# Two-layer cross-attention kernel: seven tiles of 512 rows and one of 256 instead of eight of 512, another order of the first loads and of the slot arithmetic, and two transposes placed ahead of the last gate product

## The reference, cut to what matters

```python
# layer 0, for each of 32 batches
proj = memory @ W_mem.T                                  # 375 x 512
p = softmax(x @ proj.T / sqrt(512)); mc = p @ proj
x = rmsnorm(x + sigmoid(concat(x, mc) @ W_gate.T + b) * mc)
# layer 1: a token is of expert v if it and the next one have mask 1, else of expert l
n = rms_norm(x)
qkv = where(is_v, n @ v_qkv, n @ l_qkv)                  # 512 -> 1536
q, k = apply_rotary(q, k)                                # 16 heads of 32, causal
h = x + where(is_v, ctx @ v_dense, ctx @ l_dense)
c = cross_attention(rms_norm(h) @ cq_w, encoder @ ckv_w) # 16 heads of 16
h = h + c @ cdense_w
out = h + where(is_v, mlp_v(rms_norm(h)), mlp_l(rms_norm(h)))  # 512 -> 1376 -> 512, silu(gate)*up
```

## Time and profile before

| | |
|---|---|
| median of three runs | 2606.43 us |
| profiled execution | 2607.21 us, span 2605.4 us |
| PE busy | 2340.3 us, 90% of the span |
| DVE, ACT, POOL busy | 48%, 41%, 33% |
| mean granted TensorE clock | 0.948 |
| bytes moved | 301.01 MB, 116 GB/s |

### The profile page before, as it was taken

The page is one execution under the profiler, slowest core; times in us unless marked ns, Lnnn a source line. Parts: engine busy times, 40 slices in busy tenths (PEclk is TensorE's granted clock), DMA queues, the critical chain, the costliest instruction groups (busy, mean ns, idle before and its releaser), DMA issues.

```text
span 2605.4 us, 46600 instructions
## 1 busy us (share of the span) xinstructions
PE 2340.3 (90%) x19458; PEld 1993.2 (77%) x19458; DVE 1251.0 (48%) x1871; ACT 1070.4 (41%) x1825; POOL 859.5 (33%) x720
## 2 busy tenths in 40 slices
PE   3798996999969997997999999998599999999998
PEld 2688885888858887886777777776488888888887
DVE  3455543877536663443565555565133433343332
ACT  2343424434235653442454544444334343343432
POOL 2110104666412211432121111110255646555553
PEclk7899997999979997998899999999799999999999
DMA  5343333456353333553111111110433434333341
GB/s 169 111 129 104 130 98 129 179 208 227 135 188 115 115 115 134 225 197 130 32 43 40 39 44 37 45 37 16 147 113 124 152 109 150 126 133 128 106 117 46
DMA packets 105681, 301.01 MB, mean 116 GB/s; under 512 B 14136, under 2 KB 18072, under 8 KB 98072
## 3 DMA queue, kind: packets, MB, share of 16 engines
q1 hardware_dynamic: 88128, 233.73, 27.5%
q0 software_dynamic: 17344, 64.30, 6.7%
HBM read 224.19 MB, written 73.79 MB: 114 GB/s over the span
## 4 chain that ended last, share of the span: by engine, by line
PE 80%; DVE 7%; ACT 5%; DMA 4%; issue 3%; POOL 1%; SPq 1%; POOLq 0%; DVEq 0%; ACTq 0%
PE ps L97 18%; PE ps L99 18%; PE ps L98 18%; PE ps L1048 4%; PE ps L1485 3%; PE ps L1469 3%; PE ps L1450 3%; PE ps L546 2%; ACT f_arena L1374 2%; DVE r_arena L162 2%; PE ps L1037 2%; DMA f_arena<-weights 2%; PE ps L1026 1%; PE ps L1021 1%; PE ps L1010 1%
## 5 line engine op out<-in xcount | busy, mean ns | idle before, releaser
L97 PE MATMUL ps<-r_arena 128*128 128x512 f32 (+5 forms) x2472 | 931.1, 377 | 49.9 <-DVE r_arena L604 23.3
L99 PE MATMUL ps<-r_arena 128*128 128x512 f32 (+5 forms) x2472 | 916.0, 371 | 0.0
L98 PE MATMUL ps<-r_arena 128*128 128x512 f32 (+5 forms) x2472 | 916.0, 371 | 0.0
L162 POOL TENSOR_TENSOR r_arena<-f_arena,r_arena 128x512 fp32r<-128x512 f32 (+1 forms) x438 | 581.7, 1349 | 929.1 <-ACT r_arena L184 482.5
L97 PEld LDWEIGHTS ps<-r_arena 128*128 128x128 f32 (+2 forms) x2472 | 469.8, 190 | 134.1 <-issue 52.5
L99 PEld LDWEIGHTS ps<-r_arena 128*128 128x128 f32 (+2 forms) x2472 | 467.2, 189 | 71.3
L98 PEld LDWEIGHTS ps<-r_arena 128*128 128x128 f32 (+2 forms) x2472 | 468.3, 189 | 67.8
L1556 DVE TENSOR_REDUCE e_negmax<-ps 112x3 f32<-112x1125 f32 x192 | 229.9, 1197 | 217.1 <-PE ps L1450 216.8
L184 ACT CAST r_arena<-f_arena 128x512 fp32r<-128x512 f32 x400 | 237.0, 620 | 223.3 <-PE ps L99 150.2
L1374 ACT ACTIVATE f_arena<-ps 125x1792 f32<-125x1792 f32 x96 | 159.9, 1665 | 102.4 <-PE ps L1472 102.4
L1835 DVE SCALAR_TENSOR_TENSOR f_arena<-f_arena,ps 128x512 f32<-128x512 f32 x88 | 60.4, 686 | 271.0 <-ACT f_arena L1737 271.0
(11 more groups left out here) (180 smaller groups left out, 2784.9 us busy)
## 6 DMA issues: line engine op xcount, KB each, us to landing
f_arena<-weights SPq DMA_DIRECT2D x400, 256.0 KB, 2.9
f_arena<-rows SPq DMA_DIRECT2D x16, 1160.0 KB, 5.2
f_arena<-qkv SPq DMA_DIRECT2D x32, 448.0 KB, 3.9
f_arena<-mem_e SPq DMA_DIRECT2D x32, 376.0 KB, 3.0
f_arena<-mem_t SPq DMA_DIRECT2D x16, 750.0 KB, 6.3
f_arena<-mem_n SPq DMA_DIRECT2D x8, 1500.0 KB
h_rows<-f_arena SPq DMA_DIRECT2D x8, 1160.0 KB, 4.2
f_arena<-h_rows SPq DMA_DIRECT2D x8, 1160.0 KB, 5.2
```

Of the source, the lines that this page charges most:

```text
L97: first = pe.matmul(out, w_hi, x_hi, start=start, stop=False)
L98: pe.matmul(out, w_hi, x_lo, start=False, stop=False)
L99: return first, pe.matmul(out, w_lo, x_hi, start=False, stop=stop)
L162: return engine.tensor_tensor(out, source, high.bitcast(F32), ALU.subtract)
```

## The change

The slots become 3840 (30 blocks, `BLOCKS`): seven tiles of 512 and a last one of 256. `blocks(n)` is the number of blocks before tile n, `tb(n)` the blocks of tile n: 4, and 2 for tile 7. The DRAM tensors become flat in slots. The full tiles of v are now the count of v's tokens divided by 512, rounded to the nearest; what is left of v goes into tile 7 where it didn't get a full tile. So `setup_dve_slots` has 34 operations where it had 24, and there are 256 pads to zero, 6 indirect DMAs and not 12.

```diff
+BLOCKS = BATCHES * SEQ // P + TB // 2
+SLOTS = BLOCKS * P
+PADS = TB // 2
+def blocks(n):
+    return min(TB * n, BLOCKS)
+def tb(n):
+    return blocks(n + 1) - blocks(n)
...
+        def tile_of(x, n):
+            return x[P * blocks(n):P * blocks(n + 1)].rearrange("(p j) c -> p j c", j=tb(n))
... B, and likewise D
-                    for j in range(TB):
+                    for j in range(tb(n)):
                         x = slice(j * P, (j + 1) * P)
... F, gate and up
-                        _, last = split_products(pe, ps[:, f_pair(tile, 2 + i) + up, :], whi[:, w], wlo[:, w],
-                                                 fx_hi[:, k, :], fx_lo[:, k, :], k == 0, k == KT - 1)
+                        _, last = split_products(pe, ps[:, f_pair(tile, 2 + i) + up, now], whi[:, w], wlo[:, w],
+                                                 fx_hi[:, k, now], fx_lo[:, k, now], k == 0, k == KT - 1)
```

```diff
-        def setup_sp(sp):
-            for dst, src in setups:
-                sp.dma_start(dst, src).then_inc(setup_loaded, 16)
-            for dst, src in loads:
-                sp.dma_start(dst[:], src).then_inc(const_loaded, 16)
+        def setup_act(act):
+            for dst, src in loads:
+                act.dma_start(dst, src).then_inc(const_loaded, 16)
...
-            load_x(0)
-            for c in range(CT):
-                ring_load(sp, c, weights[c])
-            load_memory_t(0)
+            ring_load(sp, 0, weights[0])
+            load_x(0)
+            ring_load(sp, 1, weights[1])
+            for t in range(CT):
+                sp.dma_start(memt_first[t], mem_t[0][:, t, :]).then_inc(a_mt_first[t], 16)
+            for dst, src in ((wm_raw, w_mem), (wg_raw, w_gate_mem)):
+                sp.dma_start(dst, src).then_inc(setup_loaded, 16)
             load_memory_n(0)
```

```diff
             u(0)
+            setup_pe(pe)
             s0(0)
-            pe.wait_ge(slots_made, 1)
+            setup_pe_wc(pe)
...
             x_low(0)
+            setup_dve(dve)
             for t in range(CT):
                 memory_low(0, t)
-            setup_dve_slots(dve)
             u_low(0)
+            setup_dve_total(dve)
+            setup_dve_weights(dve)
             softmax(0)
+            setup_dve_ranks(dve)
+            setup_dve_wc(dve)
             for g in range(GROUPS + 1):
                 if g:
                     gated(g - 1)
                 else:
-                    for t in range(CT):
-                        memory_low(1, t)
+                    attended(0, 0)
+                    attended(0, 1)
+                    memory_low(1, 0)
...
                 else:
+                    memory_low(1, 1)
                     x_low(1)
+                    setup_dve_slots(dve)
```

The transposes in A, on PE and DVE:

```diff
                 for t in range(KT):
+                    if t == KT - 1 and g + 1 < GROUPS:
+                        for b in range(2):
+                            transposed(g + 1, b)
                     if t >= 2:
                         pe.wait_ge(a_tanh, KT * g + t - 1)
...
+                    if t == KT - 1 and g + 1 < GROUPS:
+                        for b in range(2):
+                            attended(g + 1, b)
                     dve.wait_ge(a_mc_made, KT * g + t + 1)
                     dve.wait_ge(a_tanh, KT * g + t + 1)
```

More of the change, by code:

```diff
@@ L284, in setup_pe, with setup_pe_wc @@
             pe.matmul(ps[:, 5, 64:65], totals, ones_sb[0:BATCHES, 0:1], start=True, stop=True).then_inc(s_rank, 1)
+            pe.wait_ge(s_onehot, 1)
+            pe.matmul(ps[0:SEQ, 4, 128:192], onehot, table_sb, start=True, stop=True).then_inc(s_cs, 1)
+        def setup_pe_wc(pe):
+            pe.wait_ge(s_hi, KT + 1)
+            pe.wait_ge(s_lo, KT + 1)
+            for t in range(CT):
+                for k in range(KT):
+                    w = slice(t * P, (t + 1) * P)
+                    _, last = split_products(pe, ps[:, 6 + t, :], wm_hi[:, k, w], wm_lo[:, k, w],
+                                             wg_hi[:, k, :], wg_lo[:, k, :], k == 0, k == KT - 1)
+                last.then_inc(s_wc, 1)
         def setup_dve(dve):
@@ L1676, in add @@
                 pool.wait_ge(f_cd_loaded, 16 * (tile + 1))
-                for j in range(TB):
+                for j in range(tb(tile)):
                     x = f_x[tile % 3][:, j, 0:DIM]
@@ L1717, in squares @@
             def squares(tile):
-                act.wait_ge(f_added, TB * (tile + 1))
+                act.wait_ge(f_added, blocks(tile + 1))
                 if tile:
                     act.wait_ge(*f_turned.at(KT * tile))
-                for j in range(TB):
+                for j in range(tb(tile)):
                     act.activation(f_xn[:, j, :], f_x[tile % 3][:, j, 0:DIM], ACT.Square, scale=float(DIM) ** -0.5,
@@ L1749, in turn @@
                 if half == 0:
-                    pe.wait_ge(*f_normed.at(TB * (tile + 1)))
+                    pe.wait_ge(*f_normed.at(blocks(tile + 1)))
                 if tile:
@@ L1759, in gate_up @@
             def gate_up(tile, i):
+                now = slice(0, P * tb(tile))
                 if i < 2:
@@ L1819, in outputs @@
                     dve.wait_ge(*f_stored.at(16 * TB * tile))
-                for j in range(TB):
-                    if j < TB - 1:
+                for j in range(tb(tile)):
+                    if j < tb(tile) - 1:
                         dve.wait_ge(f_down_done, (TB - 1) * tile + j + 1)
```

329 lines of the change are left out of this document (176 added, 153 removed).

## The result

The changed kernel takes 2494.07 us (median of four runs, 2489.08 to 2502.27) against 2609.24 of the kernel before on the same chip: 0.957 of its time, interval 0.9545 to 0.959. The forecast was 2483, 11 us too low; the range 2465 to 2506 holds it. The profiled execution took 2494.62 us (span 2492.8).

| stretch | before | after | gain | forecast |
|---|---|---|---|---|
| start to `s0(1)` | 99.03 | 82.90 | 16.1 | 27.5 |
| `s0(1)` to B | 337.6 | 305.2 | 32.4 | 26.9 |
| B to C | 294.5 | 282.7 | 11.8 | 12.4 |
| C | 289.0 | 287.3 | 1.7 | 0 |
| D | 188.0 | 175.4 | 12.6 | 12.6 |

What follows compares the result with a forecast made beforehand. The chain that ended last was 80% PE, so fewer PE instructions, fewer pauses and a higher clock gain time. Terms 44.4 + 12.4 + 12.6 + 26.9 + 27.5 = 123.8 off 2607.2, less 0.8: 2483 us, range 2465 to 2506.

Steps and rivals of the forecast that it cites:

- The start: Time up to `s0(1)`: gain 27.5 us, at least about 20, at most 34, with `s0(1)` at 71.5.
- `s0(1)` after 80: Start: the prediction is wrong if `s0(1)` comes after 80 us; it was expected at 68 to 75.
- upper bound of 32: A, transposes ahead of the last gate product: gain 26.9 us in sum, bounds 14 and 32.
- two more signs: F's last tile: PE without pause and POOL near 0.8 busy; F's gain was put at 44.4 us.
- B and D: Half-size tile 7 in both: B gains 12.4 us (bounds 9 and 15), D 12.6 (bounds 9 and 14).
- 5.4 + 2.9 + 1.8: D, tile 7: PE time saved by fewer 512-column matmuls, fewer 256-column query matmuls, and fewer transposes, in us.
- 4.0 a group: A: gain per group, six groups, 24 us; between 4.8 if the clock stays and 2.7 at half clock.
- the last link: Start: DVE's slot operations, 11.5 us, end at 70, so `u_low(1)` is late next and `s0(1)` comes at 71.5.
- by one split per step: F, tile 7: port contention between DVE and POOL costs one split per step, 11 x 0.4 us; the sum stays.
- Rival 2: F's 256-column matmuls don't halve, paced by weight loads or by POOL through the port: 18 us less, 2501; chance 0.10.
- Chunk 10: F, tile 7, worst place for POOL: done at about 11.8 us, PE wants it at 14.2, so it holds.
- Rival 5: A: PE's clock never comes back, 24 us a group, 168 in seven; about 2630, slower than before; chance 0.01.

Runs made afterwards that it cites:

- Number 9: The changed kernel with the half tile undone (last tile four blocks again, 4096 slots, twelve pad stores): ratio 0.9825 to the kernel before.
- number 6: The changed kernel with DVE's `memory_low` in A behind the copies of all four batches: `s0(1)` to B 299.1 us, ratio 0.9554 to the kernel before.
- 8: The changed kernel with A's two transposes and two copies put back behind the last gate product: ratio 0.9693 to the kernel before.
- number 7: The changed kernel with 2 to 12 small DVE operations ahead of A's copy for b = 2: pauses 1.44 to 2.72 us, next 24 matmuls 2.93 to 4.56.
- Numbers 1: The changed kernel with DVE's setup waiting for the first five constants alone, PE for the identity: `s0(1)` at 68.04, ratio 0.9527 to the kernel before.
- 2: The changed kernel with the twelve constants issued from SP's queue behind x and the second weight chunk: `s0(1)` at 68.29, ratio 0.9514 to the kernel before.
- number 3: The changed kernel with constants in SP's queue, `mem_n` loads cut into 112 and 13 rows, slots made behind `u_low(1)`: `s0(1)` at 53.16.
- number 4: The changed kernel with one more wait of POOL in F's last tile, for `low` of h of step 3: F 699.5 us, ratio 0.9537 to the kernel before.

## Why the prediction was right, and where not

The total came out 11 us above the forecast, inside the range, but it is better than its parts. The start ended below its lower bound and met a sign that I had set for being wrong (`s0(1)` after 80: it came at 82.90), and A ended just above its upper bound of 32. These two misses partly cancel, which was luck. F missed two more signs: PE had a pause there, and POOL was 0.71 busy in the tile, not near 0.8.

*B and D* held in mechanism and size: 11.8 for 12.4, with the 5.75 us pause that ends with a rope, and 12.6 for 12.6. Number 9 shows that the tile's size makes them. That D agrees to 0.1 is partly chance. The prediction itemizes 5.4 + 2.9 + 1.8 = 10.1 us of PE (and writes 9 as its bound), doesn't show the other 2.5, and took half of the pause of 2.23 before `queries(7)` to go, where 0.63 went.

*A* was right in mechanism (1.20 us late behind `memory_low`, numbers 6 and 8). Mis-sized was the term "4.0 a group", which leaned two fifths of the way (4.8 to 2.7) to half clock behind the new pause. It measured 5.1. For 0.8 of the 1.1 number 7 shows why: 1.20 lies below the step, which is between 1.56 and 1.82 us at this place. I had only 1.89 and 3.58 to go by. The other 0.3 is that the phase up to L613 takes 8.0 us where I had added up 8.4.

*The start* failed in a step, and below my lower bound: 16.1, where "about 20" was the least. The bound took for granted that DVE would be free to run its setup; I followed the six chunks, the half contexts and ACT, but not the twelve constants, though I wrote that the trace did not show DMA issues on ACT. The twelfth landed at 36.8 us, and one wait held all of DVE's program behind it. Numbers 1 and 2 show it: either edit alone returns 14.6 to 14.9 us, more than the 11.4 missing. The slots, which I made the last link, were that: 4.99 us of pause (number 3). Their 34 operations took 9.6 us, not the 11.5 that I had counted.

*F* had the right pace, 0.120 us a matmul, and the right end. The step that failed is "by one split per step": the wait of DVE for POOL's port was priced at one split under way. In the one place where POOL ran from its stores into nine splits without a rest, it was the rest of the run: `low` took 8.21 us. That cost PE a pause of 5.09 us and 2.5 us more at half clock. With one wait of POOL, F takes 699.5, a gain of 44.8 for 44.4 (number 4). Rival 2 named the port and not this form of it. The rule of the Trainium skill that I weighed (SBUF — State Buffer, "Who interferes with whom": blocked for the whole instruction) is what 0.90 and 1.48 us show behind a rest; the 5.68, 8.21 and 12.62 us behind stores go beyond it, and there the measurement decides. Chunk 10, my worst place, did hold: PE has no pause there.

The sum of the four misses, +11.4 -5.5 +0.6 +7.8, less 3.1 that C and E gave, is 11.2 us: the whole difference between the spans.

One sum of the rivals was wrong without bearing on the result. Rival 5 added 168 us to a forecast of 2483, which is 2651 and not 2630.

## What to carry to other kernels

When loads move to another queue, look up when the last one that a wait covers will land, and give what is needed first its own semaphore or its own place in the queue. Where POOL has indirect stores and then a backlog, look whether DVE's operations with two SBUF inputs wait for the whole backlog; here one wait of POOL in between that wasn't met yet ended that. Judge a term of a few us by its stretch of the trace, since the total also carries the clock of stages that nobody touched.

## What the runs showed of the chip that I had not expected

- A 2 KB load took 30.3 us beside large loads in another queue, and 2.4 in theirs, ahead of them.
- 1500 KB in 125 rows held the start's loads back until 44 us; as 112 rows and 13 they were through by 34.
- DVE's turn behind POOL: in the one execution that tried it, a rest of 1.37 us after the indirect stores was enough. A shorter one wasn't tried.
- E, unchanged, by chip: windows rows of the changed kernel and of number 6.

```profile
1133.52:1785.11 651.59, 560.21 (x9121) 456.86 (x9121) 356.53 (x521) 294.79 (x366) 102.22 (x76) 0.96 0.16 49
```
```profile
1125.41:1823.53 698.12, 584.86 (x9120) 479.89 (x9121) 356.62 (x521) 294.88 (x366) 102.14 (x76) 0.92 0.15 45
```

DVE and ACT are as busy in both; PE's granted clock is 0.96 and 0.92, and 46.5 us lie between them.
